# A three-layer graph network on one core: every engine's list of work in a slot drawn anew

## The reference

```python
h = jnp.maximum(_layernorm(x), 0.0)                # x: (128, 128, 256)
for l in range(3):
    si, sj = x @ attn_w[l, :d], x @ attn_w[l, d:]
    scores = leaky(si[:, :, None] + sj[:, None, :] + attn_b[l], 0.2)
    attn = softmax(where(mask, scores, -inf))      # mask: adjacency + identity
    h = layernorm(x + attn @ x, g1[l], beta1[l])
    ff = gelu(h @ W1[l] + b1[l]) @ W2[l] + b2[l]   # W1: 256 x 1024
    x = layernorm(h + ff, g2[l], beta2[l])
out = input + x
```

## Time and the profile before

| | |
|---|---|
| time, median of three | 2315.44 us (2313.62 to 2316.35) |
| profiled execution: time, span | 2317.27 us, 2315.5 us |
| TensorE busy | 2247.7 us, 97% of the span |
| ScalarE, GpSimd, VectorE busy | 1905.2, 1872.8, 1793.1 us |
| TensorE's weight loads | 1575.8 us, beside its matmuls |
| DMA | 120.06 MB, 52 GB/s in the mean |

### The profile page before, as it was taken

How to read it: one execution, slowest core, us unless ns; L and a number is a source line. 1 busy time by engine, 2 the same in 40 slices (tenths; PEclk the granted TensorE clock), 3 DMA queues, 4 the chain that set the end, 5 groups by cost and what they waited for, 6 DMA issues and landing times.

```text
span 2315.5 us, 46432 instructions
## 1 busy us (share of the span) xinstructions
PE 2247.7 (97%) x15840; PEld 1575.8 (68%) x15840; DVE 1793.1 (77%) x5887; ACT 1905.2 (82%) x3496; POOL 1872.8 (81%) x1642
## 2 busy tenths in 40 slices
PE   4899999999999999999999999999999999999998
PEld 3666777776667677777666767777766677777675
DVE  7677777778887777777888877777888877777765
ACT  6778888888888888888888888888888888888874
POOL 6467877888988787878898878787989887878786
PEclk9899999999999999999999999999999999999999
DMA  6321111124442111112443111111443211111133
GB/s 180 91 65 28 24 24 24 24 42 83 96 105 47 20 28 19 29 21 53 101 100 88 33 20 28 19 29 19 83 105 88 46 24 24 26 22 28 38 69 78
DMA packets 279273, 120.06 MB, mean 52 GB/s; under 512 B 209792, under 2 KB 277376, under 8 KB 279040
## 3 DMA queue, kind: packets, MB, share of 16 engines
q1 hardware_dynamic: 263200, 101.37, 19.3%
q0 software_dynamic: 15840, 15.73, 4.6%
HBM read 49.96 MB, written 16.78 MB: 29 GB/s over the span
## 4 chain that ended last, share of the span: by engine, by line
PE 75%; DVE 12%; ACT 8%; issue 3%; DMA 1%; POOL 1%; SPq 0%; DVEq 0%; POOLq 0%; ACTq 0%
PE p_hid L417 34%; PE p_pair L431 33%; PE p_pair L477 4%; DVE g_lo L645 2%; DVE bn L652 2%; PE p_pair L455 2%; ACT probs L566 2%; PE p_pair L463 1%; DVE res L728 1%; ACT p_hid L531 1%; ACT L531 1%; DVE res L749 1%; ACT L566 1%; ACT g_hi L536 1%; DVE adj_in L673 1%
## 5 line engine op out<-in xcount | busy, mean ns | idle before, releaser
L645 DVE TENSOR_TENSOR g_lo<-p_hid,g_hi 128x512 f16<-128x512 f32 x768 | 529.9, 690 | 475.7 <-ACT g_hi L536 469.2
L431 PE MATMUL p_pair<-w_hi,g_hi 128*128 128x256 f16 x3072 | 837.9, 273 | 0.0
L431 PE MATMUL p_pair<-w_lo,g_hi 128*128 128x256 f16 x3072 | 837.8, 273 | 0.0
L431 PE MATMUL p_pair<-w_hi,g_lo 128*128 128x256 f16 x3072 | 837.8, 273 | 0.0
L531 ACT ACTIVATE p_hid<-p_hid,b_eff 128x512 f32<-128x512 f32 x768 | 505.5, 658 | 310.0 <-PE p_hid L417 308.3
L897 POOL TENSOR_TENSOR rstd<-var_eps,minus_half 128x4 f32<-128x4 f32 x224 | 236.6, 1056 | 382.9 <-DVE minus_mean L660 382.8
L536 ACT ACTIVATE g_hi<-p_hid 128x512 f16<-128x512 f32 x768 | 459.3, 598 | 24.5
L417 PE MATMUL p_hid<-hT_hi,w_hi 128*128 128x512 f16 x1536 | 458.2, 380 | 6.5 <-DMA hT_hi<-h_hi 3.5
L417 PE MATMUL p_hid<-hT_lo,w_hi 128*128 128x512 f16 x1536 | 458.7, 380 | 0.9 <-DMA hT_lo<-h_lo 0.8
L417 PE MATMUL p_hid<-hT_hi,w_lo 128*128 128x512 f16 x1536 | 458.6, 380 | 0.0
L431 PEld LDWEIGHTS p_pair<-w_lo,g_hi 128*128 128x128 f16 x3072 | 300.8, 98 | 106.7 <-issue 0.3
(11 more groups left out here) (73 smaller groups left out, 3520.2 us busy)
## 6 DMA issues: line engine op xcount, KB each, us to landing
x_in<-in_x SPq DMA_DIRECT2D x32, 512.0 KB, 3.8
out<-w_f SPq DMA_DIRECT2D x31, 512.0 KB, 5.0
w_f<-in_x POOLq DMA_DIRECT2D x30, 512.0 KB, 6.1
adj_in<-in_adj SPq DMA_DIRECT2D x32, 256.0 KB, 4.4
w_f<-in_L_gnn_W SPq DMA_DIRECT2D x6, 1024.0 KB, 6.2
hT_hi<-h_hi SPq DMA_TRANSPOSE x96, 3.1
hT_lo<-h_lo SPq DMA_TRANSPOSE x96, 3.1
g_rows<-in_L_gnn_g SPq DMA_DIRECT2D x2, 384.0 KB, 6.6
```

Of the source, the lines that this page charges most:

```text
L431: mm = pe.matmul(ff_banks(s)[:, t, :], g[i][:, nodes], w[l][:, c, :], start=(c == 0 and t % 2 == 0 and n == 0), stop=(c == C - 1 and n == ...
L645: dve.tensor_tensor(g_lo[i][:], p_hid[k][:], g_hi[i][:], ALU.subtract).then_inc(g_lo_ready, 1)
```

## The change

No operation of the steady work is added or taken away. The lists are drawn anew:

- **TensorE:** transposes of the probabilities from c=4 (ahead of the feed) to c=3 (behind the feed); the spread from c=3 to c=4; the aggregation from behind the feed of c=6 to ahead of it. The fold of a bias is done in two halves, in slots 1 and 3: one before the transposes, one before the spread.
- **VectorE:** second residual from c=2 to c=1, its statistics from c=3 to c=2, their aggregates from c=5 to c=3; add_scores from c=4 to c=3; attention residual and statistics from c=7 to c=5, their aggregates from c=0 of the next slot to c=6; dots from c=5 to c=6; mask from c=6 to c=7; statistics of an input from c=1 to c=0 and their aggregates from c=2 to c=1.
- **ScalarE:** the leaky relu stays at c=5, the exponentials go to c=6; norm_input(s+5) at c=7 becomes norm_input(s+4) at c=3.
- **GpSimd:** norm_feed and its deviation move to the next slot, directly ahead of the layer output; low_X behind both.
- **SyncE:** load of adj and the store first, the x load between the two transposes of h.
- **Opening:** inputs 2 and 3 are loaded into X[2] and X[3] and normalised there in place, so input 4 waits for input 0's norm and input 5 for input 1's; the first mask is VectorE's; every list has another order. There is one more closing slot.

```diff
-FOLD_AT = {3: 1, 5: 2}
+FOLD_AT = {4: 1, 6: 2}
...
+        def x_source(r, s):
+            return X[s] if isinstance(r, int) and r == 0 and s in (2, 3) else x_in[s % 2]
...
             def load_x(g):
-                sp.dma_start(x_in[g % 2][:], graphs(x, g)).then_inc(x_loaded[g % 2], 16)
+                dst = X[g] if g in (2, 3) else x_in[g % 2]
+                sp.dma_start(dst[:], graphs(x, g)).then_inc(x_loaded[g % 2], 16)
...
             def next_x(g):
-                sp.wait_ge(x0_ready, group_total(0, g - 2, 4, 4))
+
+                if g in (2, 3):
+                    sp.wait_ge(x_loaded[g % 2], 16)
+                else:
+                    sp.wait_ge(x_loaded[g % 2], 2 * 16)
+                    sp.wait_ge(x0_ready, group_total(0, g - 4, 4, 4))
                 load_x(g)
...
-                    if c == 4 and is_item(r, s + 2):
-                        transpose_probs(r, s + 2)
+                    if c == 6 and is_item(r, s + 2):
+                        aggregate(r, s + 2)
                     if c < LAG and is_item(r, s - 1):
                         feed(r, s - 1, C - LAG + c)
                     if c >= LAG and is_item(r, s):
                         feed(r, s, c - LAG)
 
-                    if c == 3 and is_item(r, s + 3):
+                    if c == 3 and isinstance(r, int) and r == 0 and s + 3 in FOLD_AT:
+
+                        pe.wait_ge(res2_ready, total(0, s - 1, 2, 2))
+                        fold_bias(FOLD_AT[s + 3], sj_bank(s + 3), 0)
+                    if c == 3 and is_item(r, s + 2) and not (isinstance(r, int) and (r, s) == (0, 0)):
+                        transpose_probs(r, s + 2)
+                    if c == 4 and is_item(r, s + 3):
                         spread_sj(r, s + 3)
-                    if c == 6 and is_item(r, s + 2):
-                        aggregate(r, s + 2)
                     if isinstance(r, int) and (r, s, c) == (0, 0, 0):
                         aggregate(0, 1)
+                        transpose_probs(0, 2)
...
+                    if c == 3 and is_item(r, s + 4) and layer_of(s + 4) == 0:
+                        norm_input(r, s + 4)
                     if c == 5 and is_item(r, s + 3):
+                        leaky_scores(r, s + 3)
+                    if c == 6 and is_item(r, s + 3):
                         exponentials(r, s + 3)
-                    if c == 7 and is_item(r, s + 5) and layer_of(s + 5) == 0:
-                        norm_input(r, s + 5)
...
                 norm_input(0, 0)
                 high_X(0, 0)
-                norm_input(0, 1)
+                leaky_scores(0, 0)
                 exponentials(0, 0)
                 copy_probs(0, 0)
+                norm_input(0, 1)
+                norm_input(0, 2)
                 high_weights(0, 0)
                 high_weights(0, 1)
-                norm_input(0, 2)
+                norm_input(0, 3)
                 high_X(0, 1)
-                exponentials(0, 1)
                 norm_attention(0, 0)
                 high_h(0, 0)
+                leaky_scores(0, 1)
+                exponentials(0, 1)
```

More of the change, by code:

```diff
@@ L131, in slots @@
             slot(r, s)
-    for s in range(FIRST_LOOP_SLOT, PER + 1):
+    for s in range(FIRST_LOOP_SLOT, PER + 2):
         slot(LOOPS, s)
@@ L285, in gnn_kernel @@
         pieces = [(l, n) for l in range(L) for n in range(4)]
[L287 to L288 removed]
+        act_pieces = dict(zip([(0, 6), (0, 7), (1, 0), (1, 3), (2, 0), (2, 3), (3, 0), (3, 3)], pieces[4:]))
+        dve_pieces = dict(zip([(0, 7), (1, 1), (1, 4), (2, 1), (2, 4), (2, 7), (3, 1), (3, 4)], pieces[4:]))
+        def x_source(r, s):
+            return X[s] if isinstance(r, int) and r == 0 and s in (2, 3) else x_in[s % 2]
         block = ctx.enter_context(nc.Block())
@@ L434, in feed, with fold_bias @@
                 mm.then_inc(ff_done, 1)
-            def fold_bias(l, bank):
+            def fold_bias(l, bank, half):
                 pe.wait_ge(w_dma[0], 16 * (l + 1))
                 pe.wait_ge(cols_dma, 2 * 16)
-                for c in range(C):
+                for c in range(C // 2 * half, C // 2 * (half + 1)):
                     for k in range(KD):
@@ L469, in aggregate @@
                 pe.wait_ge(X_lo_ready, total(r, s, 1, 1))
-                if is_item(r, s + 1):
+                if is_item(r, s + 1) and not (isinstance(r, int) and (r, s) == (0, 0)):
                     pe.wait_ge(score_steps, total(r, s + 1, 5, 4))
@@ L564, in exponentials @@
                     act.wait_ge(sum_steps, total(r, s - 1, 1, 1))
+                    act.wait_ge(pT_psum, total(r, s - 1, 1, 1))
                 for t in range(T):
@@ L570, in copy_probs @@
                 act.wait_ge(pT_psum, total(r, s, 1, 1))
-                act.activation(pT_hi[:].rearrange("p (t n) -> p t n", n=N), pT_bank(s), ACT.Copy).then_inc(pT_hi_ready, 1)
+                if later(r, s):
+                    act.wait_ge(agg_ready, total(r, s - 1, 1, 1))
+                act.activation(pT_hi[:], pT_bank(s), ACT.Copy).then_inc(pT_hi_ready, 1)
             def high_X(r, s):
@@ L801, in slot @@
                                               ALU.add).then_inc(last_steps, 1)
+                    if c == 2 and is_item(r, s - 1):
+                        feed_statistics(r, s - 1)
                     if c == 3 and is_item(r, s - 1):
-                        feed_statistics(r, s - 1)
+                        aggregates(2, total(r, s - 1, 10, 8))
+                    if c == 3 and isinstance(r, int) and r == 0 and s + 3 in FOLD_AT:
+                        add_bias(FOLD_AT[s + 3], sj_bank(s + 3))
+                    if c == 3 and is_item(r, s + 3):
+                        add_scores(r, s + 3)
+                        row_maxima(r, s + 3)
                     if c == 4 and is_item(r, s + 2):
@@ L838, in first_residual @@
                 attention_statistics(0, i)
+                dve.wait_ge(stat_steps[1], total(0, i, 10, 4))
+                aggregates(1, total(0, i, 10, 8))
             def opening():
@@ L976, in slot @@
                     h_residual(r, s + 1)
-                if is_item(r, s - 1):
-                    inverse_deviation(s - 1, 2, total(r, s - 1, 10, 10), total(r, s - 1, 2, 1))
-                    if not (isinstance(r, int) and (r, s) == (LOOPS, PER)):
-                        norm_feed(r, s - 1)
             def first_deviation(i, n):
```

197 lines of the change are left out of this document (99 added, 98 removed).

## The result

The changed kernel takes **2322.58 us** (median of 6 runs, 2320.92 to 2323.86), beside 2313.89 for the kernel before on the same chip (6 runs): a ratio of 1.0035, 95% interval 1.0022 to 1.0048. It is slower by a third of a per cent. Forecast were 2293 and a range of 2281 to 2303, with 7% for slower. In the later experiments the kernel before took 2316.4 us beside each run, 2.5 more than here; a difference of a run from the change, taken between medians, is therefore uncertain by about that much.

What follows compares the result with a forecast made beforehand. TensorE was taken as the bound, busy 97% of the span with 67.8 us idle. From 2315.5, 15.2 for the loop and 6.4 for the opening were subtracted, giving 2293.9, forecast as 2293 us; range 2281 to 2303.

Steps and rivals of the forecast that it cites:

- Slots with new input: VectorE's list up to the second residual, done at 10.5 against TensorE's 10.44: 0.2 us stall, 0.9 in a turn's first.
- mask 1.74: VectorE's two mask instructions in an input slot, taken as 1.74 us, the addition in it at 1.36.
- the loop's remainder: Stall left in the loop's input slots over three turns: between 0.6 and 5.7 us, taken as 3.
- Rival (4): The mask meets GpSimd nowhere or everywhere in the loop: 2291 us (15%) or 2296 us (25%).
- The loop in plain slots: Loop slots without new input: period 23.02 us, TensorE not waiting for the second residual.
- The cover of 0.9 at the aggregation's waiter: VectorE's g_lo of chunk 7, behind the aggregation, ready at 27.3, wanted by TensorE at 28.24: 0.9 us to spare.
- Rival (3): VectorE's chain behind the aggregation 1.2 us longer than counted stalls every slot: 2322 us; slower had 7%.
- GpSimd, ScalarE and the queues cost nothing: In the loop, none of their work exceeds the 23.02 us slot or delays TensorE: no cost.
- Rival (1): Transposes wait for the same late second residual, so the loop's 18.2 us of stalls stay: 2309 us, chance 5%.
- Opening at first: Slot 0 starts later, at 46.1 us instead of 42.57, behind ScalarE's norm of input 3; bounds 42.6 and 49.
- Afterwards: Slots 0 to 3: earlier load of input 5 ends waits, slot 4 starts at 163.1 instead of 169.5, 6.4 us won.
- signs of being wrong: Listed: first hidden chunk before 43 or after 49, g_lo waits at h2 every slot, late hT_lo, half clock behind fold halves.

Runs made afterwards that it cites:

- experiment 5: Changed kernel, mask moved: between second aggregates and dots at unit 6, 2296.07 us; then behind the attention statistics at unit 5, dots at unit 7, 2291.44 us.
- experiment 3: Changed kernel with the mask made at unit 5, ahead of the attention residual, instead of at unit 7: 2310.49 us, ratio 0.9975 to the kernel before.

## Why the prediction was wrong

**The step that failed** is in "Slots with new input": the term "mask 1.74", and with it the upper bound 5.7 of the loop's remainder. The addition stood in it at 1.36, its duration in most stalled slots before; the comparison, 0.43 in that slot, was counted as if it could not meet anything. The move of norm_feed by one slot was costed at nothing, and the remainder put at 3 because the addition was to meet short norm_feed operations as often as long ones: in the new order all 24 masks of the loop meet the layer output. It took 1.80 and 1.38, 3.13 us to the next g_lo. Put 1.39 more into the working: 12.0 instead of 10.65 against TensorE's 10.44 gives 1.6 us of stall; 1.5 was measured. All else in that sum stands. Of the 26.0 us between the 2293.9 of the sum and the span of 2319.9, 25.2 are this remainder, 28.2 instead of 3 (in it the two slots of 23.24 in a turn, which I didn't count). The trace of before had it: the addition of the earlier trace rows ends 0.56 behind GpSimd's operation, which is a wait that ends with the neighbour and not a slower addition; and the comparison had two durations too, 0.43 and 0.68. I compared durations only, and never laid GpSimd's timeline beside them; read so, its price is the rest of the neighbour's operation, here about 1.1 us more for the addition and 0.95 more for the comparison. Rival (4), "everywhere", was that case, mis-sized at 2296; its mechanism happened.

The Trainium skill ("SBUF — State Buffer", Who interferes with whom) says that of VectorE and GpSimd the one to issue first gets the port pair that they share for its whole instruction, and the other fully blocks; it names tensor_scalar as an operation that can contend, in a two-port mode and under conditions, beside tensor_tensor with both inputs in SBUF. The runs agree that both instructions can be held: 0.68 became 1.80, and 0.43 became 1.38 and 2.46. I used the rule for the addition only. They don't agree on the whole instruction: with the mask moved, the addition ran at 0.67 (from 1151.10) while GpSimd's deviation of four columns was under way (1150.89 to 1151.90), and at unit 6 the comparison ran at 0.43 beside such a one. Whether the comparison ran in a two-port mode, no run here shows.

**Point by point.** *The loop in plain slots:* right; 23.02 throughout, no wait for the second residual or at h2. *The cover of 0.9 at the aggregation's waiter:* right, by experiment 5. Rival (3) falls; that its 2322 is the time measured is chance, as no slot is stalled by the aggregation's waiter. *GpSimd, ScalarE and the queues cost nothing:* right of their own lengths; with the mask moved an input slot has TensorE busy for 23.03 of 23.03. *Rival (1), the stall only moves:* it is what the waits look like (same releaser, new waiter), but not its mechanism: VectorE got to the mask on time. *Opening at first:* right; slot 0 at 46.20 (46.1), first spread in it at 69.24 (68). *Afterwards:* nearly right in sum, not in its terms. Slot 4 started at 164.35, forecast 163.1, so 5.2 us were won and not 6.4. Slot 1 came at 78.8 (78.4) and slot 2 at 109.7 (109.6). Slot 2 took 24.5 where I had 23.2, since the mask stalls it as in the loop. A half of the fold took 1.84 at full clock, so 3.7 for each bias where I had 7.3, or 6.25 in the earlier trace rows; that slot 3 took 30.2 all the same, as forecast (30.3), is luck: it holds the 3.07 at 145.24 behind the long mask. Timeline of PE, a half of the last fold:

```profile
147.85 1.84 PE L457 MATMUL p_pair<-beta_col,w_f 128*128 128x1 f32 x16
```

Windows of the changed kernel:

```profile
93.24:105.24 12.00, 11.74 (x66) 7.90 (x65) 5.74 (x18) 5.96 (x12) 9.90 (x7) 0.73 0.67 177
...
125.00:155.00 30.00, 26.67 (x197) 19.43 (x195) 26.95 (x70) 24.23 (x44) 24.68 (x20) 1.00 0.35 96
```

Around the second fold the clock stays at 1.00, where the earlier trace rows had 0.83, as I thought possible; but at 93 to 105, behind the first half of the first fold and over its second, it is 0.73, which costs 3.2 us: one of my signs of being wrong. What makes it fall at one fold and not at the other was not tried. *Closing slots:* right, nothing.

## What to carry to other kernels

When an instruction of VectorE shows two durations, look at what GpSimd runs beside it, and whether it ends a constant time after GpSimd's. If so, price it as "the rest of the neighbour's operation plus most of its own time", for each instruction of the kind, also for those that happened to be cheap; and place it where GpSimd is idle. Moving a 1.1 us pair by two units (and the dots by one) was worth 31 us here, both by the medians and between the profiled executions; the whole redrawing of the lists, with the mask thinned in both kernels, 6 to 9. Of an order that depends on cover, measure the cover itself by putting a known length in front of it.

## What the runs showed of the hardware

- A mask addition of 0.68 us alone takes up to 1.59 before, 1.80 in the change and 2.82 in the run of experiment 3, by its GpSimd neighbour; a comparison of 0.43 takes 0.68, 1.38 or 2.46. Wherever one of them is longer than alone by 0.1 us or more (190 additions and 125 comparisons in the traces of all runs), the addition ends 0.53 to 0.56 us and the comparison 0.28 to 0.29 us after an operation of GpSimd. GpSimd's get longer in turn: 1.27 became 1.60 and 1.45.
- A narrow reciprocal deviation of GpSimd (128 x 4, 1.01 us) under way leaves the addition at 0.67 or 0.68 and the comparison at 0.43. The residuals, with one input in PSUM, kept 1.65 and 1.28 beside any neighbour.
- A fold's half of 16 one-column matmuls takes 3.41 us at half clock (at 19.94 in the change) and 1.84 at full.
